# Attention stage: four passes in other places, and the middle bf16 part of q and k written by GpSimd

## The reference, cut to what matters

```python
q, k, v = (x @ W.T + b).reshape(b, s, 16, 16)          # 16 heads of 16
attn_scores = einsum('bihd,bjhd->bhij', q, k) / 4
li, lj = x @ rel_W[:, :d].T, x @ rel_W[:, d:].T         # 3 relations
relation_probs = softmax(li[:, :, None, :] + lj[:, None, :, :] + rel_b)
bias = einsum('bijk,hk->bhij', relation_probs, logical_bias)
gate = sigmoid(x @ gate_W.T + gate_b)
weights = softmax(attn_scores + gate * bias)            # over j
out = einsum('bhij,bjhd->bihd', weights, v) @ Wo.T + bo
```

## Time and profile before

| | us |
|---|---|
| median of 3 runs | 6053.53 |
| lowest and highest of them | 6041.44, 6056.1 |
| the profiled execution, its own time | 6048.23 |
| its span, first to last instruction | 6046.4 |
| start of PE's last output product of the attention (L694), from the span's start | 2874.4 |

### The profile page before, as it was taken

The page is one execution under the profiler, slowest core; times in us unless marked ns, Lnnn a source line. Parts: engine busy times, 40 slices in busy tenths (PEclk is TensorE's granted clock), DMA queues, the critical chain, the costliest instruction groups (busy, mean ns, idle before and its releaser), DMA issues. The chain is left out here.

```text
span 6046.4 us, 122850 instructions
## 1 busy us (share of the span) xinstructions
PE 5371.3 (89%) x40162; PEld 3536.9 (58%) x40162; DVE 4703.6 (78%) x6099; ACT 4404.3 (73%) x7005; POOL 3700.2 (61%) x2010
## 2 busy tenths in 40 slices
PE   6888888888888898888799869999999979999999
PEld 4666666666666666655344345555555546666665
DVE  6999999999999999998898679999999942122221
ACT  4999999999999999999366678888888821111111
POOL 3888888888888888775100069999999930000000
PEclk8999999999999999999899889999999989999999
DMA  2121121212112121200355555565555531111110
GB/s 76 26 50 30 28 52 28 52 28 51 28 35 45 31 49 31 44 19 13 123 197 213 185 211 185 210 207 189 197 202 209 180 106 40 47 35 35 35 35 11
DMA packets 461360, 538.76 MB, mean 89 GB/s; under 512 B 237536, under 2 KB 337760, under 8 KB 460784
## 3 DMA queue, kind: packets, MB, share of 16 engines
q1 hardware_dynamic: 460784, 531.75, 28.1%
HBM read 370.31 MB, written 161.35 MB: 88 GB/s over the span
## 5 line engine op out<-in xcount | busy, mean ns | idle before, releaser
L502 DVE CUSTOM_DVE_ANT_0 srow<-srow,ps_s,small 128x1024 f32<-128x1024 f32 x1024 | 1305.0, 1274 | 71.6 <-issue 49.8
L576 ACT ACTIVATE srow<-srow,nmax 128x1024 f32<-128x1024 f32 x1024 | 1199.7, 1172 | 94.8 <-DVE nmax L502 83.0
L585 ACT COPY AT<-ps_t 128x512 f32<-128x512 f32 x2048 | 1110.6, 604 | 24.2 <-PE ps_t L658 23.4
L658 PEld LDWEIGHTS ps_t<-ident,srow 128*128 128x128 f32 x8192 | 959.2, 141 | 222.6 <-issue 16.8
L658 PE MATMUL ps_t<-ident,srow 128*128 128x128 f32 x8192 | 1077.1, 274 | 2.8 <-ACT AT L585 2.4
L1977 POOL TENSOR_TENSOR c_hc<-c_hs,c_cs 128x1024 f32<-128x1024 f32 x432 | 1010.1, 2365 | 63.9 <-DVE c_hs L2079 62.1
L491 DVE SCALAR_TENSOR_TENSOR srow<-ps_p,rho,R 128x1024 f32<-128x1024 f32 x768 | 976.0, 1271 | 0.0
L1938 PE MATMUL c_ps_y<-c_hc,c_ident 128*128 128x512 f32 x2048 | 945.9, 595 | 30.0 <-POOL c_hc L1977 17.1
L2079 DVE TENSOR_TENSOR_SCAN c_hs<-c_da,c_pd 128x1024 f32<-128x1024 f32 x384 | 859.8, 2274 | 58.0 <-PE c_pd L1929 54.6
L647 PE MATMUL ps_s<-K,Q 96*128 96x512 bf16 x2048 | 621.3, 385 | 286.8 <-DVE nmax L502 271.5
L2022 ACT ACTIVATE c_sT<-c_dxT,c_bT 128x256 f32<-128x256 f32 x1536 | 668.4, 494 | 105.7 <-PE c_pd L1929 95.7
(11 more groups left out here) (256 smaller groups left out, 8571.8 us busy)
## 6 DMA issues: line engine op xcount, KB each, us to landing
c_cs<-bc_d SPq DMA_DIRECT2D x256, 512.0 KB, 4.2
c_bs<-bc_d SPq DMA_DIRECT2D x64, 512.0 KB, 6.6
Q<-parts_d SPq DMA_DIRECT2D x384, 64.0 KB, 2.2
parts_d<-parts SPq DMA_DIRECT2D x57, 384.0 KB, 3.3
K<-parts_d SPq DMA_DIRECT2D x168, 128.0 KB, 4.3
sz_d<-b_sz SPq DMA_DIRECT2D x16, 1024.0 KB, 7.2
xv_d<-b_xv SPq DMA_DIRECT2D x16, 1024.0 KB, 7.9
dt_d<-b_ab SPq DMA_DIRECT2D x16, 1024.0 KB, 4.2
```

What stands on the lines that cost most here:

```text
L502: nc.vector.tensor_tensor_reduce(r[:], r[:], ps_s[:], small[:, slot, h:h + 1], BIG, ALU.add, ALU.min, nmax[:, h % NROW:h % NROW + 1]).then ...
L576: nc.scalar.activation(r[:], r[:], ACT.Exp, scale=-1.0, bias=nmax[:, h % NROW:h % NROW + 1]).then_inc(e_ok, 1)
L585: nc.scalar.copy(AT[h % NAT][:, HG * half:HG * half + HG, :], ps_t[:, half]).then_inc(at_ok, 1)
L658: last = nc.tensor.transpose(ps_t[:, half, i, :], rows_sb[h % NROW][:, j * P:(j + 1) * P], ident[:])
```

## The change

POOL writes the middle part itself, as a subtraction with a bf16 result, ahead of the one that forms the remainder in f32; ACT's cast is gone, and `pool_lo` waits for both of POOL's own steps. On DVE, step 0 of `dve_rel` goes from behind head 0's `dve_s` to ahead of it, and `dve_v` from behind head 4 to behind head 5 and `dve_xn`. On ACT, step 1 of `act_y0` goes from behind head 8's exponential to ahead of it, and `act_o` from behind head 5's exponential to ahead of it.

```diff
         def pool_rem(pool, p):
             alone(pool, hi_ok, p + 1, pool_own)
+            nc.gpsimd.tensor_tensor(parts[:, 1], qkf[:], parts[:, 0], ALU.subtract).then_inc(mid_ok, 1)
             nc.gpsimd.tensor_tensor(qkf[:], qkf[:], parts[:, 0], ALU.subtract).then_inc(rem_ok, 1)
 
         def pool_lo(pool, p):
             alone(pool, mid_ok, p + 1, pool_own)
+            alone(pool, rem_ok, p + 1, pool_own)
...
-        def act_mid(act, p):
-            wait(act, rem_ok, p + 1)
-            nc.scalar.copy(parts[:, 1], qkf[:]).then_inc(mid_ok, 1)
...
             def body(dve, t, k, par, ib, pro, post, look, before):
+                if look:
+                    dve_rel(dve, t + 1, 1 - k, after(par, ib, 1), 0)
                 for u in range(H):
...
-                    if look and u < 2:
-                        dve_rel(dve, t + 1, 1 - k, after(par, ib, 1), u)
+                    if look and u == 1:
+                        dve_rel(dve, t + 1, 1 - k, after(par, ib, 1), 1)
...
-                    if pro and u == 4:
+                    if pro and u == 5:
                         dve_v(dve, t + NT, 1 - par, ib)
...
             def body(act, t, k, par, ib, pro, post, look, before):
                 for u in range(H):
+                    if look and u == 8:
+                        act_y0(act, t + 1, 1)
                     act_e(act, t, u)
-                    if post and u == 5:
-                        act_o(act, t - 1)
...
-                    if look and u in (7, 8):
-                        act_y0(act, t + 1, u - 7)
+                    if look and u == 7:
+                        act_y0(act, t + 1, 0)
...
-                    if followed(t, pro) and u == 2:
-                        act_mid(act, t - 1 + AHEAD)
...
+                    if post and u == 4:
+                        act_o(act, t - 1)
```

More of the change, by code:

```diff
@@ L1073, in start @@
                 act_g_ge(act, 1)
-                act_mid(act, NT)
                 act.wait_ge(g_st, 16 * 8)
```

## The result

| | us |
|---|---|
| changed kernel, median of 4 runs | 6230.84 (6225.99 to 6233.96) |
| kernel before on the same chip, median of 4 runs | 6054.32 (6041.44 to 6056.1) |
| ratio, 95% interval | 1.0301 [1.0286, 1.0316] |
| profiled execution of the changed kernel, its span | 6228.8, 6226.8 |

The change makes the kernel slower by 3.0%, 177 us. The forecast had the direction right and 97 us against the profiled execution, just over half of the loss; the time lies above the range, which ended at 6178.

The account below looks back on a forecast made before the run. Each attention tile was taken as a DVE loop of three legs, the first bounded by POOL's and ACT's chain: 29.3 + 9.78 + 5.94 = 45.0 us against 43.15. Over 55 tiles +104, less 8: 6048.2 becomes 6145, range 6045 to 6178.

Parts of the forecast that it names:

- s0: Start of head 0's score step on DVE; one tile runs from one such start to the next, 43.15 us before.
- The port-sharing alternative: DVE and POOL share the port at half speed each: moved step takes twice 0.55, tile 43.65, sum about 6068.
- third leg: End of head 14's score step to next head 0 score step: 3.91 us before, forecast 5.94 with moved step held.
- first leg: Head 0's score step to the Newton step: 29.46 us before, forecast 29.3, set by POOL's chain or DVE held at xn.
- the forecast's 104 less 8: Attention: +1.9 us a tile over 55 of 64 tiles gives +104 us; waits at batch changes give back 8.
- Worth nothing: V moved behind xn on DVE: its wait of 0.39 us is filled, but POOL holds DVE later, so no gain.
- the coin flip: At xn, DVE or POOL's head 8 addition first, equally likely: Newton step at 29.2 or 29.5; 29.3 taken.
- The 8 us for the changes of batch: Six batch changes where head 0 waits 2.05 us for keys instead of 0.28; later start absorbs most, -8 us.
- The last tiles, taken as 0: Step already held in the last tiles; a longer hold replaces another: between -4 and +4 us, taken as 0.
- The rivals: DVE first, 6022 to 6045, chance 0.10; every gap won, 5987, 0.06; POOL not bounding first leg, 6050 to 6068, 0.06.
- DVE did not go first at head 0: Rival: moved step passes ahead of POOL's head 4 addition in 0.55 us; tile 42.7 to 43.1, 6022 to 6045; chance 0.10.
- POOL did bound the tiles: Rival denied this: step 0 held, DVE's own 27.8 us sets the Newton step; 6050 to 6068 us; chance 0.06.

Follow-up runs that it names:

- the kernel with PE busy at both holds: Changed kernel plus unused identity transposes on PE, 16 in pe_aT and 10 in pe_oT, ahead of their own: 6168.6 us, ratio 1.0213 to the kernel before.
- The three single edits: Kernel before with one edit each: middle part on POOL without the cast, 1.011; step 0 ahead of head 0's score step, 1.0162; V behind head 5 and xn, 1.0096.
- V alone: Kernel before with only dve_v moved behind head 5 and dve_xn: 6107.51 us, ratio 1.0096.
- PE busy at step 0's hold: Changed kernel plus 16 unused identity transposes on PE in pe_aT, ahead of its own two: 6210.83 us, ratio 1.0274 to the kernel before.

## Why the prediction was right in direction and wrong in size

**What held, to a tenth.** The moved step is held by POOL's addition: head 14's end at 1060.41 to the next s0 at 1066.35 is 5.94, as forecast, and the step's mean is 2.48 for "near 2.4". ACT waits 2.23 ahead of head 0's exponential, against 0.22 in the tile before the change, where the forecast had some 2 more:

```profile
1067.66 1.15 ACT L574 ACTIVATE srow<-srow,nmax 128x1024 f32<-128x1024 f32 x1 [2.23 <-DVE nmax L504]
```

The Newton step to head 14's end is 9.76 (9.78 forecast). POOL's L384 starts at s0 + 6.98 (7.00), L372 takes 1.44 here and 1.29 in the mean (1.6), L373 1.16 (1.15). Where xn is free and the clock full, the tile is 44.61 (44.6) and the Newton step waits 0.9 for POOL. Where xn is held and the clock full, the tile of the kernel with PE busy at both holds is 45.42, a first leg of 29.7 for 29.5 to 29.8. The port-sharing alternative, by which the third leg would be 4.57, falls by the 5.94: the trace agrees with the lock that the Trainium skill states ("SBUF — State Buffer", Who interferes with whom).

**The step that failed: the clock.** The prediction read a granted clock of 1.00 in the earlier trace rows, as a property of the stage, and carried it over to the changed kernel. No term, no rival and no bound priced a lower one. But the same text forecast ACT, and with it PE's chain, to wait 2 us more each tile; the next question, what PE does in that time, was not asked. With PE's idle pieces of 2.56 and of 1.27 and 1.74, part of most tiles runs at half clock, and late scores then make DVE wait, the engine that sets the tile. Of the +3.02 a tile, the kernel with PE busy at both holds has 1.95 (45.47 against 43.52 in the mean), and about 1.07 is left for the clock; over 55 tiles that is 107 and 59 us. The first is close to the forecast's 104 less 8, in part by luck: the forecast took xn held and xn free as equally likely, and at full clock 46 tiles had it held and 6 free. The range's upper end, 6178, was made of full-clock cases alone, so it could not hold the time.

The trace of before had this price already, at a row that the prediction read. The xn of 2.09 us at 717.05 was taken for the hold alone. PE's timeline behind it, and the stretch between the Newton steps around it, in the columns of the earlier trace rows:

```profile
719.43 0.63 PE L680 MATMUL ps_m<-ident,O 128*128 128x128 f32 x4 [0.76 <-ACT O L589]
721.59 0.68 PE L647 MATMUL ps_s<-K,Q 96*128 96x512 bf16 x2 [1.53 <-DVE nmax L502]
722.06 1.91 PE L658 MATMUL ps_t<-ident,srow 128*128 128x128 f32 x8
```

```profile
686.06:732.78 46.72, 39.62 (x462) 29.95 (x461) 43.39 (x59) 42.39 (x65) 35.49 (x23) 0.96 0.11 27
```

That tile took 46.72 us instead of 43.15, with the clock at half behind the held xn. To follow one hold through the whole tile, on PE too, would have shown what it costs.

**A second, smaller step: V.** "Worth nothing" and "29.3" for the coin flip was wrong in what it left out. That xn would be held at 29.5 to 29.8 was one of the two sides, and it came in 33 tiles of 55. But the moved V costs 1.0% by itself, on the kernel before: 1.29 us a tile in the mean, of which 0.42 stands at full clock too (43.56 against 43.14); the rest goes with half clock.

**Two small terms.** The 8 us for the changes of batch rested on one row. In the trace of before only two of the six have a wait of some 2 us ahead of head 0 (2.05 and 1.92), the others 0.28 or 0.29, so it was at most 4. The last tiles, taken as 0, cost 5. Neither bears on the miss.

**The rivals.** None came true. DVE did not go first at head 0, as step 0's mean shows; POOL did bound the tiles in which xn is free, and DVE the others, where L484 waits for nothing.

**What stays open.** The three single edits add up to 3.7% and together cost 3.0%, as they can share holds and half-clock stretches; a division of the 3.0% among them is not unique. Tiles of 45.4 and 46.9 stand side by side in one execution; they differ in the hold behind which the clock fell, but why it fell behind the one and not the other is open. What the fills at the two holds cost by themselves was not measured, and since xn is held in more tiles with them than without, 107 and 59 us divide the loss between two kernels, not within one.

## What to carry to other kernels

A forecast that adds a wait to the leading engine has to ask what the tensor engine does in that wait, even if it is busy 88% and not the bound: idle pieces of some 2 us took its clock to half here, and the late results come back to the leading engine as a second wait. When two engines lock each other out, place each instruction by its distance from the other's passes, and go on to the next pair behind it, because every shift moves that one too. Where the order is good but leaves a hole on the tensor engine, a few useless products in the hole can be worth about the whole hole: here the ratio is 1.0173 without them and 0.9945 with them, some 2 us a tile for a hole of 2.04, between two kernels that differ in nothing else.

## What the runs showed of the hardware

- PE's clock fell to its half level (1.2 GHz) behind idle pieces of 1.3 to 2.6 us, in a stage in which PE is busy 87%. Eight transposes then take 1.78 to 1.91 us instead of 1.04, the four products L692 1.92 instead of 1.03. A single stretch costs the tile 1.1 us (V alone) to 1.6 us (PE busy at step 0's hold).
- Not each such piece does it: the 2.56 ahead of head 1's scores at 1067.68 left the clock at full in that tile, and 2.57 one tile earlier did not (the transposes behind it took 1.91). What else decides was not settled.
- A tie goes to POOL here: xn and POOL's addition both start at 1080.97 in the trace, POOL keeps its 2.36, and xn takes 2.51. In the changed kernel this holds for all 23 pairs in which the addition starts between 0.03 us before xn and 0.06 after it; in the 5 pairs in which it starts 0.14 to 0.28 after it, xn goes first and takes 0.41.
- The hold doesn't depend on how small the held instruction is: xn, 128x256 with 0.41 of its own, stands for 2.51, and step 0, four times as large, for 2.46.
